# One fused conv/scan/attention kernel on Trainium2: the order of work on four engines, rewritten as a table of words per step

## The reference

```python
x = L0(x)   # whitening of groups of 4 channels over the whole batch, then a 4x4 mix: an affine map per point
# L1, per image, 1024 points in a row:
xn = (x - mean) * rsqrt(var + 1e-5) * ln_w + ln_b          # over the 128 channels
xi, z = split(W_in @ xn)                                   # 256 + 256 rows
xc = silu(causal_conv4(xi));  dt, B, C = split(W_x @ xc)
delta = softplus(W_dt @ dt + b_dt)
h[l] = h[l-1] * exp(delta * A_n) + delta * xc * B_n[l]     # 16 states n, 256 rows
y = sum_n h * C_n + xc * D;  x1 = W_out @ (y * silu(z)) + x
# L2, per image: attention over 1024 points
x2 = gamma * softmax(q.T @ k) @ v + x1
# L3, per image: attention again, then batch norm over the whole batch
f = conv_w @ (softmax(theta.T @ phi / sqrt(128)) @ x2);  out = batchnorm(f) * g + b + x2
```

## Time and profile before

| | before |
|---|---|
| median of 3 runs | 5769.74 us (5769.5 to 5771.86) |
| profiled execution | 5763.95 us, of which the span of the trace 5762.1 |
| PE busy | 4653.2 us (81%) |
| DVE busy | 4746.2 us (82%) |
| ACT busy | 3719.3 us (65%) |
| POOL busy | 4722.2 us (82%) |
| granted TensorE clock | 0.962 of full, mean |

### The profile page before, as it was taken

One profiled execution on the slowest core, in us unless ns is written; L12 is line 12 of the kernel. 1 busy time (PEld: TensorE's weight loads), 2 busy tenths in 40 slices (PEclk: granted clock), 3 DMA queues, 4 the chain that ended last, 5 costly groups with the idle time before them and its releaser, 6 DMA issues.

```text
span 5762.1 us, 62166 instructions
## 1 busy us (share of the span) xinstructions
PE 4653.2 (81%) x17331; PEld 2660.0 (46%) x17331; DVE 4746.2 (82%) x5978; ACT 3719.3 (65%) x6077; POOL 4722.2 (82%) x3342
## 2 busy tenths in 40 slices
PE   6578888888888888888888888888888888888871
PEld 6234454444444444544444444445444444444441
DVE  4688888888888888888988888888889888888823
ACT  3466667666666766666666667666666676666633
POOL 0698988888888888888888888898889899888910
PEclk9689999999999999999999999999999999999995
DMA  4455655655566555555555655565565556555517
GB/s 130 183 223 220 227 206 218 220 218 202 219 220 219 204 220 223 209 213 222 218 198 219 224 216 207 220 225 201 213 224 218 208 216 228 216 201 216 221 66 295
DMA packets 199100, 1216.88 MB, mean 211 GB/s; under 512 B 27880, under 2 KB 28656, under 8 KB 67696
## 3 DMA queue, kind: packets, MB, share of 16 engines
q1 hardware_dynamic: 194416, 1196.26, 55.8%
q10 hardware_dynamic: 4352, 16.78, 0.7%
HBM read 1158.43 MB, written 54.53 MB: 211 GB/s over the span
## 4 chain that ended last, share of the span: by engine, by line
PE 55%; ACT 22%; DVE 10%; issue 9%; POOL 3%; DMA 1%; SPq 0%; DVEq 0%; ACTq 0%; POOLq 0%
PE psT L828 24%; PE psE L828 17%; PE psT L1006 8%; ACT da L694 6%; ACT p L740 6%; DVE hs L497 4%; PE psY L828 4%; ACT pt L704 3%; DVE nm L522 1%; ACT L663 1%; POOL pa L301 1%; ACT L763 1%; ACT sz L666 1%; DVE psD L484 1%; PE psD L828 1%
## 5 line engine op out<-in xcount | busy, mean ns | idle before, releaser
L301 POOL TENSOR_TENSOR pa<-hs,rows_all 128x1024 f32<-128x1024 f32 x1024 | 2412.3, 2356 | 397.4 <-DVE hs L497 397.4
L694 ACT ACTIVATE da<-delta,neg_a 128x512 f32<-128x512 f32 x2048 | 1367.7, 715 | 97.2 <-DVE hs L497 86.5
L307 POOL TENSOR_TENSOR pa<-pa 128x512 f32<-128x512 f32 x1024 | 1308.0, 1277 | 40.1
L484 DVE TENSOR_TENSOR psD<-rows_all,psU 128x512 f32<-128x512 f32 x2048 | 1306.4, 683 | 4.4 <-DMA rows_all<-bc_scratch 4.2
L497 DVE TENSOR_TENSOR_SCAN hs<-da,hlast,psD 128x512 f32<-128x512 f32 x1024 | 1265.6, 1265 | 4.2 <-ACT da L694 4.2
L497 DVE TENSOR_TENSOR_SCAN hs<-da,psD 128x512 f32<-128x512 f32 x1024 | 1204.0, 1205 | 3.8 <-ACT da L694 3.8
L704 ACT ACTIVATE pt<-psT 128x512 f32<-128x512 f32 x1024 | 609.9, 596 | 907.1 <-PE psT L1006 903.9
L522 DVE TENSOR_REDUCE nm<-psE 128x1 f32<-128x1024 f32 x512 | 622.1, 1215 | 621.8 <-PE psE L828 621.8
L828 PE MATMUL psT<-pt,va 128*128 128x256 f32 x4096 | 1009.3, 393 | 133.9 <-DVE x L540 75.2
L828 PEld LDWEIGHTS psT<-pt,va 128*128 128x128 f32 x4096 | 767.4, 195 | 400.1 <-issue 125.0
L1006 PE MATMUL psT<-ident,p 128*128 128x128 f32 x4096 | 646.2, 281 | 331.8 <-ACT pt L704 217.7
(11 more groups left out here) (181 smaller groups left out, 4872.5 us busy)
## 6 DMA issues: line engine op xcount, KB each, us to landing
rows_all<-bc_scratch SPq DMA_DIRECT2D x1024, 1024.0 KB, 4.7
xin<-x SPq DMA_DIRECT2D x40, 512.0 KB, 7.8
xres<-x SPq DMA_DIRECT2D x64, 256.0 KB, 6.2
x_scratch<-x SPq DMA_DIRECT2D x32, 512.0 KB, 5.5
f_scratch<-fa SPq DMA_DIRECT2D x32, 512.0 KB, 6.9
xres<-x SPq DMA_DIRECT2D x8, 512.0 KB, 3.6
x1g<-x SPq DMA_DIRECT2D x8, 512.0 KB, 3.6
fa<-x SPq DMA_DIRECT2D x8, 512.0 KB, 3.6
```

The source lines that it names most:

```text
L301: pool.tensor_tensor(pa[:, k % PROD, :, :], hs[:, sl, :, :], rows_all[:, slot, 2:4, :], ALU.mult).then_inc(S["prod"], 1)
L307: pool.tensor_tensor(pa[:, k % PROD, 0, :], pa[:, k % PROD, 0, :], pa[:, k % PROD, 1, :], ALU.add).then_inc(S["pair"], 1)
L484: dve.tensor_tensor(psD[:, j, :], rows_all[:, slot, j, :], psU[:, :], ALU.mult).then_inc(S["dbu_ok"], 1)
L694: act.activation(da[:, k % 2, j, :], delta[:, h, cols(ch)], ACT.Exp, scale=neg_a[:, h, 2 * q + j:2 * q + j + 1]).then_inc(S["da_ok"], 1)
```

## The change

The tables of step numbers go, and four tables of words come, one for each engine, 16 lines for the 16 steps of a chunk. Each `image` reads its line word by word; a number at a word's end is the tile, group or half. The words for the halves are now separate: `turna`/`turnb`, `copya`/`copyb`, `weigha`/`weighb`, and also each single decay, scan, silu and z. The waits in the called functions are as before, apart from following their instruction.

```diff
-        TILE_AT = [7, 8, 10, 11, 13, 14, 16, 17]
-        TURN_AT = [8, 10, 12, 12, 14, 15, 17, 18]
-        RECIP_AT = [10, 13, 15, 18]
-        WEIGH_AT = [(11, 12), (14, 15), (17, 18), (19, 19)]
-        ATTEND_AT = [13, 16, 18, 20]
...
+        ORDER_PE = [
...
+            "key energy0",
...
+        ORDER_ACT = [
...
+            "decay0 copya0 exp1 decay1 copyb0 silu0 silu1 z1 z0",
...
-                            if scan:
-                                scan_state(b, k, 1)
-                            for a, o in now:
-                                row_max(a, o)
-                                attended(a, o)
+                            for word in ORDER_DVE[r].split():
+                                what, n = parts(word)
+                                if what == "dbu" and scan:
+                                    spread_inputs(b, k)
+                                if what == "scan" and scan:
+                                    scan_state(b, k, n)
...
+                                if what == "max" and now:
+                                    row_max(*now, n)
```

More of the change, by code:

```diff
@@ L244, in build @@
-        LATE = 5
-        AT_C, AT_N, AT_X, AT_Z, AT_B, AT_P = 0, 3, (5, 6), 9, 10, 11
-        AT_R = 3
+        LATE = 5
+        ORDER_PE = [
+            "centre variance",
+            "energy7 add turna6 weigha2 turnb6",
+            "weighb2 resx turna7 residual",
+            "turnb7 weigha3 weighb3 query add",
+            "",
+            "inner0 add inner1",
+            "key energy0",
+            "add",
+            "values energy1 turna0",
+            "gates1 turnb0 skip0 add energy2 gates0",
+            "rows turna1 turnb1",
+            "energy3 steps0 add",
+            "weigha0 steps1 weighb0 turna2 energy4 turnb2 turna3 skip1 turnb3",
+            "add",
+            "energy5 turna4 weigha1 turnb4 weighb1",
+            "turna5 energy6 turnb5 add",
+        ]
@@ new lines, in build @@
+        ORDER_DVE = [
+            "dbu scan0 scan1 max6",
+            "dbu scan0 attend1 scan1 gate1",
+            "dbu max7 scan0 scan1",
+            "dbu recip3 attend2 scan0 normed scan1",
+            "dbu scan0 scan1 attend3",
+            "dbu scan0 scan1",
+            "dbu scan0 scan1",
+            "dbu scan0 inputs scan1 max0",
+            "dbu scan0 scan1 max1",
+            "dbu scan0 scan1",
+            "dbu scan0 max2 scan1",
+            "dbu gate0 scan0 scan1 max3",
+            "dbu recip0 scan0 recip1 scan1",
+            "dbu scan0 scan1 max4 attend0",
+            "dbu scan0 scan1 max5",
+            "dbu scan0 inputs recip2 scan1",
+        ]
@@ L251, in cols, with attention, front_part @@
+        def attention(b, c, r, att, late):
+            if r >= LATE or c == 1:
+                return (b - 1, c if r >= LATE else 0) if att else None
+            return (b - 2, 1) if late else None
+        def front_part(b, c, scan, more):
+            return (b, 1) if c == 0 and scan else (b + 1, 0) if c == 1 and more else None
         def cols(c):
@@ L792, in _ @@
+                FRONT_ACT = ("centre", "rstd", "xi", "silu", "z", "table", "rows", "sp", "ln")
+                for r in range(NS):
+                    for word in ORDER_ACT[r].split():
+                        what, n = parts(word)
+                        if what in FRONT_ACT:
+                            front(what, n, 0, 0)
+                for j in range(2):
+                    decay(0, 0, j)
                 image(0, True, True, False, False)
@@ L1080, in image @@
                     for c in range(NCH):
[L1081 to L1086 removed]
+                        front_of = front_part(b, c, scan, more)
+                        old = attention(b, c, 0, att, late)
                         beside, now_att = {}, {}
```

474 lines of the change are left out of this document (224 added, 250 removed).

## The result

The changed kernel takes **5247.09 us** (median of 6 runs, 5245.52 to 5247.9), the kernel before in the same comparison 5770.15 (6 runs, 5759.08 to 5773.73). The ratio is 0.9095 with a 95% interval of 0.9083 to 0.9107; 5262 was forecast, with a range of 5210 to 5420. The profiled execution took 5247.66 us, of which the span 5245.8.

A forecast was written before the change was run, and what follows sets the result against it. No engine was full: VectorE waited for TensorE's energies, GpSimd for VectorE's scan. Profiled 5763.95 - 488 (main part) - 20 (last stretch) = 5256; the runs' median lies 5.8 above the profiled one, so 5262 us; range 5210 to 5420.

The forecast's parts named there:

- The two meet: Steady image after the change: VectorE's work and waits, 149 us, against GpSimd's 149.45; GpSimd never starves, smallest lead 1.75 us.
- The main part: First product of image 1 to last of image 31: 5146.4 us becomes 4659, 488 us less, at 150.45 an image.
- The 1 us of missed margins: Estimated 1 us an image, added to GpSimd's 149.45, for places where margins of 0.1 to 0.7 us are missed.
- VectorE's waits: VectorE in a chunk: waits about 2 us in place of 11, giving 149 us an image with its work.
- 8.8 us in place of 11.4: TensorE, steps 12 and 13: energy3 to energy4 without waits, so the 3.17 us wait before max4 goes.
- Energy3: Step 11: exp2 no longer waits for the second copy, energy3 ends before it is asked for; the 3.13 us wait goes.
- The port: VectorE and GpSimd's shared port lock could hold xn for a whole product; trace read as a delay under half of one.
- rival of xn: Xn loses to products and holds GpSimd: 4 us an image, 1 covered, about 93 us more, 5355 us; 6%.
- The closed chain: TensorE or ScalarE 2 to 3 us late in steps 8 to 14: VectorE bounds, 156 us an image, 5430; 14%.
- The ring: Max, exp, second copy, turned half, energy, max wait on each other, steps 8 to 14: slower, 6090 us; 4%.
- The last stretch: Attention alone, 5488 to 5645 us: from 40 us less to 10 more, taken as 20 less.
- The clock: Granted clock 0.98 of full over an image, 0.72 behind a stand of TensorE; no loss and no gain counted.

The follow-up runs named there:

- e12: Kernel before the change, GpSimd's sum of two pairs in odd steps over 256 of 512 columns: 5771.14 us, 166.85 an image.
- e7: Changed kernel, GpSimd's sum of two pairs in odd steps over 256 of 512 columns: 5200.07 us, 149.08 an image.
- e5: Changed kernel, xn in the images multiplies by psU in PSUM instead of rstd in SBUF: 5212.79 us, 149.31 an image.
- e2: Changed kernel, both copies of a tile together again on ScalarE, exps 1, 2, 4, 5 and 7 behind them: 5486.94 us, 157.63 an image.
- e11: e2 with both decays ahead of the copies in steps 9, 10, 13 and 14: 5469.52 us, 157.21 an image.
- e8: Changed kernel, max7 and max2 back at the ends of steps 1 and 10: 5243.2 us, 150.26 an image.
- e4: Changed kernel, values back ahead of energy0, ScalarE's words to match: 5254.89 us, 150.52 an image.
- e1: Changed kernel, energy4 back behind turned halves and skip on TensorE, weigha0 ahead of steps1: 5425.24 us, 156.14 an image.
- e3: Old order on all four engines, but new lines for TensorE's steps 11 and 12 and ScalarE's 10 to 13: 5501.82 us, 158.16 an image.
- e6: Changed kernel, xn in step 3 right behind the inputs dbu, before recip3 and attended group 2: 5233.58 us, 149.94 an image.

## Why the prediction was right, and where not

- **What bounds the kernel.** Right, and shown: e12 takes 8.7 us an image from GpSimd before the change and gains nothing, e7 does so after it and gains 1.25 us until VectorE is reached. "The two meet" is right as well, and nearer than forecast: the smallest lead was to be 1.75 us, before the product of step 15, and is 0.1 us, before that of step 3, where the long xn stands between the scans.
- **The main part.** 488 us less were forecast (487 by its own numbers), 495.1 measured; 150.45 us an image against 150.33.
- **The 1 us of missed margins** is a right number with a wrong reason, and so in part luck. GpSimd idles 8.0 us in all before its products, 0.15 in a steady image, and not 1. The rest of the 0.88 us over the 149.45 of image 0 is in its own instructions. In e5 xn costs GpSimd nothing, and an image takes 149.31 us where image 0 of e5 takes 148.66: 0.6 us an image for operations that are all some nanoseconds longer in the steady images (a product 9 ns). No run explains that remainder. About 1.0 us an image (150.33 - 149.31) goes to xn; 0.8 of it (149.45 - 148.66) was already inside my 149.45.
- **VectorE's waits.** 2 us a chunk forecast, 1.9 measured, at other places. The layout is for chunk 1, but the waits that it was set against (1.66, 3.13, 3.17) are of a chunk 0; in chunk 1 max0 didn't wait before the change either, and max3 and max4 waited 2.6 and 2.9. Max0 was forecast 0.95 and measured 0.40 in chunk 0 and none in chunk 1; attended group 0 1.0 and 0.9. Max4 was forecast without a wait and has 1.11 and 0.50. The failed step is "8.8 us in place of 11.4": from start to start, my own distances for energy3, steps0, add, weigha0, steps1, weighb0, rinv and turna2 are 1.9 + 1.05 + 0.86 + 1.83 + 1.05 + 1.83 + 0.44 + 0.44 = 9.4, not 8.8, and the trace shows 9.51 (2501.09 - 2491.58). With 9.4 the layout puts energy4's end at 63.35, 0.5 us late, which is what chunk 1 shows (0.51). The other 0.6 us of chunk 0 the layout doesn't have.
- **Energy3.** Right: its max no longer waits (2493.72), and e2 and e11 show the reason: with the exps behind the second copies max3 waits again and the image costs 6.9 to 7.3 us more. I had not priced that move by itself and in e2 took it for at most half of this.
- **The maxima's new places and values' place** are worth less than can be told from no change (e8 -4 us, e4 +8 us against the changed kernel): VectorE's lead covers them. What was shown to do work is energy4's place on TensorE (e1) and the exps' on ScalarE (e2, e11); the places of energies 5 to 7 are argued, from the waits that e3 leaves before max5 to max7, and were not tried by themselves.
- **The port.** Here I was wrong. I read "a delay of less than half of one" from xn's median of 1107 ns and let it speak against the rule. But xn met a whole product already then; it was short only because it started 1.8 us into it (1764.08 and 1762.21 above), and the place between the scans starts it 0.5 us into it (medians of 62 instances each). So xn's length could have been forecast from the trace of before: what is left of GpSimd's instruction, plus 0.55 us. Its median rose to 2413 ns, above the 2 us that I had named as the sign. The product that runs holds xn to its end, xn then holds the next pair sum, and e5 shows the cause, since one input in PSUM takes all of it away. The Trainium skill ("SBUF — State Buffer", section "SBUF: two separate sides") says that the shared port pair is an exclusive lock, which the one that starts first keeps for its whole instruction. The trace agrees: in both kernels xn ends 0.55 us behind the end of the product beside it. The rival of xn nevertheless didn't come true in its price, 4 us an image, 3 of them uncovered: it costs VectorE 1.3 us a chunk, which uses up its lead at step 3 to the last 0.1 us but hardly more (GpSimd idles 0.15 us an image), and e6, which brings the median back to 1072 ns, gains 0.4 us an image.
- **The other rivals.** The closed chain is e2 and e11: 157 and 158 us an image for the forecast's 156, but in the changed order of ScalarE's words it isn't there. The ring is open as well: the turned halves that wait have no urgent energy behind them.
- **The last stretch.** 20 us less forecast, 23.6 measured. Image 0 is as it was (149.6 against 149.45), and the first product of image 1 is 2.4 us later; no run was made for either.
- **From the profiled execution to the median** I added 5.8 us. After the change the two differ by 0.6. Without that term the sum was 5256, 9 us above the measured median, and with it 15. The upper end of the forecast, 5330, doesn't follow from its own terms: 152.45 us an image and nothing won at the end make 5345. Nothing hangs on it.
- **The clock.** I counted neither loss nor gain. The granted clock of a steady image is 1.00 for 0.98, the mean of a weighing matmul is 381 ns for 393 (pages of the two kernels), and TensorE is busy 138.0 us an image for 140.2 (means of images 1 to 30). VectorE waited for energies before the change, so some of the 16.1 us may come from these 2.2; no run tells that part from what the places of the words give by themselves.

## What to carry to other kernels

Where no engine is full, look for the producer that stands behind work that nobody is waiting for yet (here an energy behind turned halves and an exp behind a copy), and forecast the period from the busiest engine's own stretch without the others, plus what is left of the waits. Read the waits of every kind of chunk, not of one. Add the distances between two such producers twice, since the margins are of the size of one small instruction, and put moved words back in small groups: here one energy cost 5.8 us an image and a group of five exps 6.9, while two other groups cost nothing that could be seen. An instruction of VectorE like xn, with two SBUF inputs, belongs beside a short instruction of GpSimd or late in a long one, and before a move changes that, look at what runs beside it and not only at its median. Taking an independent small instruction (0.18 us) from between two dependent ones of GpSimd gained nothing.
